# Recurrent heads as f32 products of four heads each, in one stage of a sixteen-layer kernel

## The reference, cut to what matters

```
x = rmsnorm(layernorm(h)) * norm_w             # 128 channels, 16 heads of 8
s[t] = tanh(s[t-1] @ tanh(a[head]) + x[t, head] @ b[head])    # state of 64 numbers, s[-1] = 0
y[t] = s[t] @ c[head] + skip * x[t]
h = h + layernorm(h) + y @ w_out + b_out
```

## Time and profile before

| | |
|---|---|
| median of 3 runs | 3547.36 us (3545.41 to 3551.08) |
| span of the profiled execution, first to last instruction | 3541.9 us |
| stage of the change, first step to the last | 827.0 to 1475.2 us, 648.2 us for 512 steps |
| behind the last step, to the next layer | 1475.2 to 1487.1 us |
| mean granted TensorE clock, whole span / these steps | 0.886 / 0.50 |
| busy in the whole span: PE, DVE, ACT, POOL | 90%, 62%, 50%, 29% |

### The profile page before, as it was taken

One profiled execution on the slowest core, in us unless ns is written; L12 is line 12 of the kernel. 1 busy time (PEld: TensorE's weight loads), 2 busy tenths in 40 slices (PEclk: granted clock), 3 DMA queues, 4 the chain that ended last, 5 costly groups with the idle time before them and its releaser, 6 DMA issues. The chain is left out here.

```text
span 3541.9 us, 57755 instructions
## 1 busy us (share of the span) xinstructions
PE 3172.6 (90%) x21270; PEld 1680.4 (47%) x21277; DVE 2204.9 (62%) x5867; ACT 1780.1 (50%) x4015; POOL 1035.8 (29%) x454
## 2 busy tenths in 40 slices
PE   8888899997888888898989898988889898999998
PEld 3333344445777777643433343333334344556447
DVE  5777445446666666666478702889980166963991
ACT  3555423424444444426377524777752455753762
POOL 1111100000000000000089501999960103960990
PEclk8999999996555555699989999999999999999999
DMA  5443331120000000030400000000000200231124
GB/s 149 108 104 89 97 93 41 56 78 25 3 3 3 3 3 3 2 98 1 170 0 1 0 0 0 1 1 1 0 1 0 87 1 21 87 155 72 71 96 178
DMA packets 76776, 168.46 MB, mean 48 GB/s; under 512 B 9552, under 2 KB 46544, under 8 KB 67920
## 3 DMA queue, kind: packets, MB, share of 16 engines
q1 hardware_dynamic: 76496, 164.78, 14.2%
HBM read 120.70 MB, written 44.04 MB: 47 GB/s over the span
## 5 line engine op out<-in xcount | busy, mean ns | idle before, releaser
L1249 PE MATMUL psum<-h_ring,h_parts 128*128 128x4 bf16 (+2 forms) x12288 | 418.0, 170 | 121.3 <-ACT h_ring L1337 121.3
L2273 DVE TENSOR_TENSOR_SCAN s_hh<-psum,s_dbu 128x512 f32<-128x512 f32 x384 | 445.5, 1207 | 41.0 <-ACT psum L2098 39.6
L2185 POOL TENSOR_TENSOR s_dbu<-s_du,s_bb 128x1024 f32<-128x1024 f32 x190 | 443.0, 2358 | 43.8 <-ACT s_bb L2081 43.8
L1249 PEld LDWEIGHTS psum<-h_ring,h_parts 128*128 128x128 bf16 x12288 | 372.3, 105 | 171.1 <-ACT h_ring L1337 145.0
L1959 PE MATMUL psum<-s_term,w_c 128*128 128x512 f32 x768 | 405.8, 616 | 4.2 <-POOL s_term L2192 4.2
L1337 ACT ACTIVATE h_ring<-h_pre 128x16 f32<-128x16 f32 x1024 | 168.3, 211 | 357.6 <-DVE h_pre L1399 357.6
L2098 ACT ACTIVATE psum<-s_delta,s_decay 128x512 f32<-128x512 f32 x384 | 261.6, 690 | 65.8 <-DVE s_hh L2273 65.5
L901 POOL MEMSET r_weights<- 128x512 f32 x4 | 2.1, 525 | 930.1 <-POOLq L1222 660.5
L910 DVE TENSOR_TENSOR f_hid<-f_gate,psum 128x512 f32<-128x512 f32 x184 | 126.6, 688 | 204.8 <-PE psum L836 198.0
L1399 DVE TENSOR_REDUCE h_pre<-psum 128x16 f32<-128x48 f32 x1024 | 165.0, 203 | 141.7 <-PE psum L1249 141.7
L897 ACT ACTIVATE f_gate<-psum 128x512 f32<-128x512 f32 x184 | 109.7, 597 | 281.6 <-PE psum L832 281.4
(11 more groups left out here) (495 smaller groups left out, 6380.0 us busy)
## 6 DMA issues: line engine op xcount, KB each, us to landing
x_spill<-x_flip SPq DMA_DIRECT2D x28, 1024.0 KB, 3.8
f_share<-f_wide SPq DMA_DIRECT2D x208, 128.0 KB, 3.0
a_ks<-a_spread SPq DMA_DIRECT2D x96, 128.0 KB, 3.3
a_qs<-a_spread SPq DMA_DIRECT2D x96, 128.0 KB, 3.9
x_spare<-x_spill SPq DMA_DIRECT2D x4, 2048.0 KB, 7.7
x_raw<-x_spill SPq DMA_DIRECT2D x4, 2048.0 KB, 7.6
x_norm<-x_spill SPq DMA_DIRECT2D x4, 2048.0 KB, 7.6
w_l3f<-in_l3f SPq DMA_DIRECT2D x1, 7240.0 KB, 21.2
```

Source lines behind the costliest of these rows:

```text
L1249: mm = nc.tensor.matmul(columns_of(s // BLOCK, grp)[:, s % BLOCK, 0:3 - part, cols], parts[:, part, GROUP * grp + p, :], upper[:, (s - 1) ...
L2185: nc.gpsimd.tensor_tensor(dbu[:, s % D_RING], du[:, t % 2], both(bb[:, s % B_RING, :]), ALU.mult).then_inc(dbu_ready, 1)
L2273: nc.vector.tensor_tensor_scan(hh[:, s % 4, half, :], DECAYS[i % 3], dbu[:, s % D_RING, half, :], 0.0, ALU.mult, ALU.add).then_inc(scan_do ...
```

## The change

All the recurrent arithmetic becomes f32. Four heads lie in the four 64x64 quadrants of one 128x128 array, so 16 heads are 4 arrays (`QUADS`). A head's state lies in one half of the partitions and its columns are zero in the other half, so a product of 16 columns (4 heads x 4 sequences) gives each head its result in one half and an unused number in the other. Because the result comes out in another half than the state went in, odd steps use a second set of arrays in which the middle two heads are exchanged (`turned`). A group is now 2 arrays and 32 columns (`COLS`). ScalarE takes tanh straight from PSUM into `ring`, for each group in two operations, one for each half of the partitions (16 columns on 64 partitions). The sum and the remainders go, the bf16 matrices too. The core of the diff:

```diff
-        for grp in range(2):
-            pe.wait_ge(state[grp], n)
-            add_part(2, s, grp)
-        for grp in range(2):
-            pe.wait_ge(rest[grp], n)
-            add_part(1, s, grp)
-        for grp in range(2):
-            pe.wait_ge(last[grp], n)
-            add_part(0, s, grp).then_inc(drive[grp], 1)
+    def advance(i, grp):
+        for q in range(GROUP):                       # GROUP = 2
+            cols = slice(q * 4 * BATCH, (q + 1) * 4 * BATCH)
+            mm = nc.tensor.matmul(columns_of(i // BLOCK, grp)[:, i % BLOCK, cols], at[:, i % 2, GROUP * grp + q, :],
+                                  ring[:, (i - 1) % TURN, grp, cols], start=False, stop=True, skip_group_check=True)
+        mm.then_inc(drive[grp], 1)
...
+    for i in range(TIME):
+        blk, s = divmod(i, BLOCK)
+        piece, place = divmod(i, PIECE)
+        if s in (2, 3) and blk + 1 < BLOCKS:
+            lay_inputs(blk + 1, s - 2)
+        if piece and place in MIX_AT:                # s >= 4: four of eight steps
+            mix_in(piece - 1, MIX_AT.index(place))
+        if i % SPAN == SPAN // 2 and i > SPAN:
+            project_out(i // SPAN - 1)
+        warm(nc, g, bank[7], 1)
+        for grp in range(2):
+            if i:
+                pe.wait_ge(state[grp], 2 * i)
+            advance(i, grp)
```

```diff
 # ScalarE
-        act.wait_ge(summed[grp], n)
-        nc.scalar.activation(ring[:, (n - 1) % TURN, grp, 0, :], pre[:, grp, :], ACT.Tanh).then_inc(state[grp], 1)
-    if s == 1 and blk:
-        keep(blk - 1)
-    if blk + 2 < TIME // BLOCK:
-        put(blk + 2, s)
+        act.wait_ge(drive[grp], i + 1)
+        for half in range(2):
+            rows = slice(S * half, S * half + S)
+            nc.scalar.activation(valid(ring[rows, i % TURN, grp, :], i % 2, half),
+                                 valid(columns_of(blk, grp)[rows, s, :], i % 2, half), ACT.Tanh).then_inc(state[grp], 1)
```

More of the change, by code:

```diff
@@ L1187, in recurrent_heads @@
     nc, bank, w = g.nc, g.bank, g.w["l1a"]
-    PAIRS, S, BLOCK = 8, 64, 8
-    GROUP = PAIRS // 2
-    WIDTH = GROUP * BATCH
+    HEADS, QUADS, S, BLOCK = 16, 4, 64, 8
+    GROUP = QUADS // 2
+    COLS = GROUP * 4 * BATCH
     TURN = 2 * BLOCK
[L1192 to L1203, removed]
+    BLOCKS, SPAN, PIECE = TIME // BLOCK, 128, 32
+    PAIRS = GROUP * 2
+    MIX_AT = tuple(s for s in range(PIECE) if s % BLOCK >= 4)
+    with stage(g, InnerNorm.SEMAPHORES + " weights_bounded squared ms_ready logged rms_ready x_ready cleared "
+                  "laid_free laid drive0 drive1 state0 state1 kept mix_ready mix_kept out_ready biased resid_done") as (sb, sems):
+        (weights_bounded, squared, ms_ready, logged, rms_ready, x_ready, cleared,
+         laid_free, laid, drive0, drive1, state0, state1, kept, mix_ready, mix_kept, out_ready, biased, resid_done) = sems[6:]
+        drive, state = (drive0, drive1), (state0, state1)
+        at = sb("h_at", [P, 2, QUADS, P])
         sq = sb("h_sq", [P, TOKENS])
@@ L1237, in _, with lay_inputs @@
                 pe.wait_ge(norm.normed, CHUNKS)
-                def lay_inputs(blk, grp, n):
-                    pe.wait_ge(laid, n)
-                    nc.tensor.matmul(columns_of(blk, grp)[:, :, 0, :], w["b"], lay[:, blk, grp, :, :],
+                def lay_inputs(blk, grp):
+                    pe.wait_ge(laid, blk + 1)
+                    nc.tensor.matmul(columns_of(blk, grp), w["b"], lay[:, blk % 2, grp, :, :],
                                      start=True, stop=True).then_inc(laid_free, 1)
[L1245 to L1252, removed]
@@ new lines, in mix_in @@
+                def mix_in(piece, n):
+                    if n == 0:
+                        pe.wait_ge(kept, (piece + 1) * PIECE // BLOCK)
+                    parity, p = n // (2 * PAIRS), n % (2 * PAIRS)
+                    first, per = piece * PIECE, SPAN // PIECE
+                    home = bank[4 + piece // per % 2].rearrange("p (t b) -> p t b", b=BATCH)
+                    if n == 0 and piece % per == 0 and piece >= 2 * per:
+                        pe.wait_ge(resid_done, piece // per - 1)
+                    mm = nc.tensor.matmul(home[:, piece % per * PIECE + parity:(piece % per + 1) * PIECE:2, :],
+                                          w["c"][:, (parity * 2 * PAIRS + p) * P:(parity * 2 * PAIRS + p + 1) * P],
+                                          hist[:, first + parity:first + PIECE:2, p // PAIRS, p % PAIRS * BATCH:(p % PAIRS + 1) * BATCH],
+                                          start=(p == 0), stop=(p == 2 * PAIRS - 1))
+                    if n == 4 * PAIRS - 1:
+                        mm.then_inc(mix_ready, 1)
@@ new lines, in project_out @@
+                def project_out(c):
+                    pe.wait_ge(mix_kept, c + 1)
+                    nc.tensor.matmul(bank[4 + c % 2].rearrange("p (b t) -> p b t", b=BATCH), w["out"],
+                                     mix[:, :, c * SPAN:(c + 1) * SPAN], start=True, stop=True).then_inc(out_ready, 1)
+                pe.wait_ge(rms_ready, CHUNKS)
+                for grp in range(2):
+                    lay_inputs(0, grp)
+                pe.wait_ge(weights_bounded, 1)
+                pe.wait_ge(cleared, 1)
@@ L1288, in _ @@
[L1288 to L1291, removed]
+                        if i:
+                            pe.wait_ge(state[grp], 2 * i)
+                        advance(i, grp)
+                warm(nc, g, bank[7], 4)
+                for n in range(4 * PAIRS):
+                    mix_in(TIME // PIECE - 1, n)
@@ L1293, in _ @@
+                warm(nc, g, bank[7], 4)
+                project_out(TIME // SPAN - 1)
             @block.sync
@@ L1314, in _ @@
                 act.wait_ge(cleared, 1)
-                def keep(blk):
-                    for grp in range(2):
[L1317 to L1332, removed]
+                for i in range(TIME):
+                    blk, s = divmod(i, BLOCK)
                     if s == 0 and blk >= 2:
@@ L1364, in _ @@
                 dve.wait_ge(g.loaded["l1a"], 16)
-                for sem in state + rest + last:
-                    nc.vector.memset(g.mark, 0.0).then_inc(sem, 1)
-                    dve.wait_ge(sem, 1)
-                dve.wait_ge(cleared, 1)
                 def square(j):
@@ L1420, in add_input, with keep @@
-                def add_input(j):
-                    nc.vector.tensor_tensor(fixed(g.resid, j), fixed(g.resid, j), fixed(g.normed, j), ALU.add).then_inc(biased, 1)
-                for c in range(TIME // SPAN):
+                def add_input(j):
+                    nc.vector.scalar_tensor_tensor(out=fixed(g.resid, j), in0=fixed(g.normed, j), scalar=w["b_out"],
+                                                   in1=fixed(g.resid, j), op0=ALU.add, op1=ALU.add).then_inc(biased, 1)
+                def keep(blk):
+                    for grp in range(2):
+                        dve.wait_ge(state[grp], 2 * (blk + 1) * BLOCK)
+                    first = blk % 2 * BLOCK
+                    for parity in range(2):
+                        for half in range(2):
+                            rows = slice(S * half, S * half + S)
+                            src = ring[rows, first + parity:first + BLOCK:2, :, :].rearrange("p t g c -> p t (g c)")
+                            dst = hist[rows, blk * BLOCK + parity:(blk + 1) * BLOCK:2, :, :].rearrange("p t g c -> p t (g c)")
+                            if parity == 0:
+                                src = src.rearrange("p t (k u b) -> p t k u b", u=2, b=BATCH)[:, :, :, half, :]
+                                dst = dst.rearrange("p t (k b) -> p t k b", b=BATCH)
+                            else:
+                                src = src.rearrange("p t (q v c) -> p t q v c", q=QUADS, v=2)[:, :, :, half, :]
+                                dst = dst.rearrange("p t (q c) -> p t q c", q=QUADS)
+                            done = nc.vector.tensor_copy(dst, src)
+                    done.then_inc(kept, 1)
@@ L3244, in weight_parts, with turned @@
     n = "L1_attn_a_"
-    c_own = np.concatenate([blocks((P, P), [(64 * s, 8 * (2 * p + s), a[n + "c"][2 * p + s]) for s in range(2)])
-                            for p in range(8)], axis=1)
-    a_two = np.concatenate([blocks((P, P), [(64 * s, 64 * s, a[n + "a"][2 * p + s]) for s in range(2)]) for p in range(8)], axis=1)
-    b_two = blocks((P, P), [(8 * h, 64 * (h % 2), a[n + "b"][h]) for h in range(16)])
-    parts["l1a"] = [("a", a_two), ("b", b_two),
+    quads = [[4 * q + k for k in range(4)] for q in range(4)]
+    def turned(q, parity):
+        h0, h1, h2, h3 = quads[q]
+        return (h0, h1, h2, h3) if parity == 0 else (h0, h2, h1, h3)
+    c_own = np.concatenate([blocks((P, P), [(0, 8 * low, a[n + "c"][low]), (64, 8 * high, a[n + "c"][high])])
+                            for parity in range(2) for q in range(4)
+                            for low, high in ((lambda t: ((t[0], t[1]), (t[2], t[3])))(turned(q, parity)))], axis=1)
```

(4 more changed lines are left out.)

114 lines of the change are left out of this document (40 added, 74 removed).

## The result

| | before | after |
|---|---|---|
| median, same chip (4 runs each) | 3549.22 us | 4155.94 us (4148.77 to 4158.92) |
| ratio | | 1.1706, 95% interval 1.1689 to 1.1723 |
| span of the profiled execution | 3541.9 us | 4153.7 us |
| steps | 648.2 us | 1254.5 us |
| last step to the next layer | 11.9 us | 13.4 us |

A forecast was written before the change was run, and what follows sets the result against it. The chain of a step bounded the old kernel, TensorE at the low clock the new one. Steps grow from 648.2 to 1258.2 us (+ 610.0), with the ends + 614: span 4156, time 4162 us, range 4110 to 4280.

The forecast's parts named there:

- The clock: Granted clock in the recurrent steps: they begin low, at 0.50 (1.2 of 2.4 GHz), and do not lift it.
- Rival A: Clock 1.00 in nearly all steps, plain step 1.05 us, 3553 us in all, not slower; chance 0.07.
- The f32 load: Short f32 weight load with its product on TensorE: 0.214 us at the low clock, 0.112 at the high one.
- Rival C: Low clock, but short f32 loads stay at 0.11 us: plain step 1.24 us, 3730 us in all; chance 0.04.
- The step: Recurrent step with TensorE never pausing: plain 1.96 us at the low clock; all 512 steps together 1258.2 us.
- Lay and mix: On TensorE, `lay_inputs` adds 1.03 us in 126 steps and `mix_in` 0.505 us in 240, no longer hidden in idle time.
- The hidden work: Per 8 steps, VectorE's four copies (at most 4 x 0.29 us) and GpSimd's two operations (under 2) hide in 19.7 us.
- The ends: Outside the steps: first lay + 0.9 us, behind the last step + 1.4, next layer's low-clock start + 2 (0 to 6).
- The tanh operations: On ScalarE, two in a row take 0.33 us, four about 0.45; in time with 0.27 us to spare.
- 5.5 us from span to time: Median of the runs stands 5.5 us above the profile's span, taking 4156 to 4162 us.

The follow-up runs named there:

- burst run: The changed kernel with 16 more unused products of 512 columns straight ahead of the first step, the one in each step kept: 4140.6 us.
- bf16 run: The changed kernel with recurrent matrices in one bf16 part, states' upper halves as operand, remainders left out, unused product kept: 3352.1 us, repeated 3344.6 us, ratio 0.9432.

## Why the prediction was right, point by point

- **The clock.** Forecast: the new steps arrive low and do not lift it. Shown: 0.50 over 1254 us, and the burst run shows that they would also let a high clock fall within 9 us. Rival A's price for a plain step was near (1.05 forecast, 1.09 measured at 1.00); its condition was not met. The Trainium skill's advice to keep TensorE busy without long idle gaps (TensorE: Matmul & The Clock Gate, "Why this matters for your kernels") does not decide such a stage: TensorE's records filled 1088 of 1088 us in the run without the unused product, at clock 0.50. Why the clock stays low there, and what exactly three unused products bring that one does not, these runs do not take apart.
- **The f32 load.** Forecast 0.214 us at the low clock. In the changed kernel seven loads take 1.62 us, (1.62 - 0.33)/6 = 0.215 (timeline of the weight loads below). Rival C is out. The Trainium skill's price for a load (same page, "LDWEIGHTS (loading the stationary operand)"), 107 ns with no word on the clock, agrees with 0.112 at 1.00 alone.
- **The step.** Plain 1.96 forecast, 1.95 measured; with mix 2.46 forecast, 2.45 measured; with lay 2.99 forecast, 2.99 measured. The steps together 1258 forecast, 1254.5 measured.
- **Lay and mix, free before, paid for now.** The forecast charged 251 us for them. Steps with mix were 0.5 us longer than plain ones and steps with lay 1.04, and TensorE has no idle time in which they could lie.
- **The hidden work.** VectorE's copies took 0.93 us for four, GpSimd's operations 0.63 us each; of ScalarE's idle time 1.1 us was due to the copies.
- **The ends.** Last step to the next layer + 1.4 forecast, + 1.5 measured (11.9 to 13.4). The next layer began at the low clock. Of the rest of the difference between the spans, some 4 us, 0.6 lie ahead of the first step and 3.4 from the next layer on; 3 were forecast, 0.9 and 2.
- **The tanh operations.** This price was mis-sized and hidden: a pair takes 0.38 us, not 0.33, and four cover 0.8 us, not 0.45. It decided nothing here; in the bf16 run the four are the bound.

```profile
1100.02 1.62 PEld L1247 LDWEIGHTS psum<-h_ring,h_at 128*128 128x128 f32 x7
```

The sum came out 2 us from the span (4156 against 4153.7) and 6 from the median. The difference is one more term that was wrong: 5.5 us from span to time, where the median was of three executions and the span of one. Wherever a run has both numbers for the same execution, the time stands 1.9 to 2.1 us above the span (4155.6 against 4153.7). That the total is this close is in part luck: the kernel before measured 3535 to 3558 us from run to run. One reading behind the choice of the clock was a shade off as well: the longest idle piece of the old stage is 0.51 us, not under 0.5, which changes nothing.

The last lines of TensorE in the stage show the end as forecast, 32 short records of 0.214 us at the low clock:

```profile
2083.97 7.09 PE L1261 MATMUL psum<-h_hist,w_l1a 128*128 128x64 f32 x32
2090.85 1.91 PE L65 MATMUL psum<-c_bf 128*128 128x512 bf16 x4
2092.55 1.92 PE L1270 MATMUL psum<-h_mix,w_l1a 128*128 128x512 f32 x2
```

## What to carry to other kernels

Count the weight loads before the columns: in a chain of short products, 8 f32 loads cost more here than 24 bf16 loads at either clock (0.97 us, in the run with the burst, against 0.76 at 1.00; 1.83, in the run without the unused product, against 0.73 at 0.50), so fewer and wider products in f32 can lose to many in bf16. Read the granted clock of the stage before pricing f32 work on TensorE, and take prices from rows at that clock. Filler work for the clock is not a safe gain: one unused product in a step was pure cost here (166 us), two lost the clock after 260 us, three kept it where the stage began high and did not lift it for over 1000 us where it was low.

## What the runs showed of the hardware that I had not expected

- A bf16 weight load with its product of 4 to 12 columns costs about the same at both clocks: 0.027 us at 0.50, 0.029 at 1.00 (0.76 us for 24). An f32 load with its short product takes half the time at twice the clock, 0.214 and 0.112 us. The Trainium skill has a floor between starts of short products of about 25 ns (TensorE: Matmul & The Clock Gate, "Wait — 56ns, not 53.3ns?"), with which the first agrees.
- The clock had a memory: the same steps with three unused products ran at 1.00 for 860 us after a dense start, and at 0.50 for over 1000 us after a low one.
- Two tanh operations of 64 partitions x 16 numbers from PSUM follow each other by 0.20 us, two of 128 x 16 from SBUF by 0.12. Whether that is the source, the partitions or the way in which the numbers lie is not shown.
